# Convolution of a gated cross-attention block: four summands per output position instead of two go from GpSimd to the identity products on TensorE

## The reference

```
kv = vr[:, :, :, None, :] * x2r[:, :, None, :, :]        # (B, 16, i=8, j=8, 256)
y = irfft(rfft(kv, n=512) * rfft(k, n=512))[..., :256]     # causal convolution with k
y = y + kv * skip
out = einsum('bhijl,bhil->bhjl', y, x1r)                  # sum over the eight i
x = x + tanh(g) * out.reshape(B, 128, 256)
```

## Time and profile before

| what | value |
|---|---|
| median of three executions | 913.87 us |
| span of the profiled execution | 913.1 us |
| its median's distance from that span | 0.8 us |
| stage A, up to the last a_sum's start | 0 to 171.66 us |
| from there to the first matmul of the experts | 171.66 to 179.94 us |
| the rest | 179.94 to 913.10 us |
| mean granted TensorE clock | 0.957 of full |

### The profile page before, as it was taken

How to read it: one execution, slowest core, us unless ns; L and a number is a source line. 1 busy time by engine, 2 the same in 40 slices (tenths; PEclk the granted TensorE clock), 3 DMA queues, 4 the chain that set the end, 5 groups by cost and what they waited for, 6 DMA issues and landing times.

```text
span 913.1 us, 13862 instructions
## 1 busy us (share of the span) xinstructions
PE 823.8 (90%) x4659; PEld 653.9 (72%) x4675; DVE 619.3 (68%) x1196; ACT 320.9 (35%) x515; POOL 173.7 (19%) x185
## 2 busy tenths in 40 slices
PE   2888888699999999999998999987789999999994
PEld 2565666588888878888884555555678888888883
DVE  5999999564565465466547778788256685867754
ACT  2120212123433342342334776756243332324221
POOL 1899999400000000020000100100010010100000
PEclk9999999899999999999999999997579999999997
DMA  7221211000000000001001122110000000000000
GB/s 266 70 87 46 72 45 62 18 1 1 1 0 0 0 0 0 0 0 35 15 1 47 52 56 73 52 39 1 0 1 0 1 12 12 0 23 0 23 1 24
DMA packets 20437, 25.93 MB, mean 28 GB/s; under 512 B 3632, under 2 KB 15920, under 8 KB 20272
## 3 DMA queue, kind: packets, MB, share of 16 engines
q1 hardware_dynamic: 20400, 25.47, 8.7%
HBM read 23.36 MB, written 2.10 MB: 28 GB/s over the span
## 4 chain that ended last, share of the span: by engine, by line
PE 72%; DVE 17%; issue 6%; ACT 2%; POOL 1%; DMA 1%; DVEq 0%; SPq 0%; POOLq 0%; ACTq 0%
PE bank L1556 24%; PE bank L1426 19%; PE bank L1439 10%; PE bank L1477 5%; PE bank L1487 2%; DVE A L854 2%; DVE A L843 2%; PE bank L1565 2%; PE bank L1497 1%; PE bank L1351 1%; DVE small L1048 1%; DVE A L1058 1%; PE bank L1352 1%; PE bank L1353 1%; PE bank L1478 1%
## 5 line engine op out<-in xcount | busy, mean ns | idle before, releaser
L1556 PE MATMUL bank<-R 128*128 128x512 f32 (+4 forms) x1104 | 220.0, 360 | 9.7 <-DVE R L1210 4.9
L1556 PEld LDWEIGHTS bank<-R 128*128 128x128 f32 (+2 forms) x1104 | 180.7, 185 | 48.5 <-DVE R L1210 5.1
L1426 PE MATMUL bank<-R 128*128 128x512 f32 (+1 forms) x816 | 198.0, 392 | 1.9 <-issue 1.9
L1426 PEld LDWEIGHTS bank<-R 128*128 128x128 f32 (+1 forms) x816 | 146.7, 185 | 33.2 <-issue 2.1
L995 DVE TENSOR_TENSOR A<-bank,A 128x512 f32<-128x512 f32 (+1 forms) x68 | 47.0, 691 | 118.7 <-PE bank L1426 118.7
L1439 PEld LDWEIGHTS bank<-R 128*128 128x128 f32 (+1 forms) x816 | 105.8, 190 | 10.8 <-issue 4.0
L1439 PE MATMUL bank<-R 128*128 128x256 f32 (+1 forms) x816 | 109.4, 283 | 2.5 <-DVE R L1006 2.1
L558 ACT ACTIVATE A<-bank 128x512 f32<-128x512 f32 (+1 forms) x68 | 40.7, 599 | 194.7 <-PE bank L1426 194.7
L1477 PE MATMUL bank<-A 128*128 128x512 f32 x128 | 70.9, 636 | 0.8
L1351 PE MATMUL bank<-A 128*128 128x256 f32 x128 | 45.4, 439 | 26.0 <-DVE A L843 17.9
L430 POOL TENSOR_TENSOR A<-A 128x256 f32<-128x256 f32 x64 | 64.1, 1002 | 11.5 <-DVE A L854 11.5
(11 more groups left out here) (170 smaller groups left out, 1138.4 us busy)
## 6 DMA issues: line engine op xcount, KB each, us to landing
A<-in_w SPq DMA_DIRECT2D x17, 384.0 KB, 3.1
A<-in_w SPq DMA_DIRECT2D x8, 480.0 KB, 3.7
A<-in_ctx_one SPq DMA_DIRECT2D x8, 272.0 KB, 3.6
A<-in_ctx_half SPq DMA_DIRECT2D x8, 256.0 KB, 3.1
A<-in_ctx_nat SPq DMA_DIRECT2D x4, 512.0 KB, 3.6
A<-in_ctx_t SPq DMA_DIRECT2D x128, 16.0 KB, 2.0
out<-X SPq DMA_DIRECT2D x4, 512.0 KB, 2.9
A<-in_filt SPq DMA_DIRECT2D x1, 1536.0 KB, 11.8
```

The lines of the kernel that those rows point to most:

```text
L1426: mm = nc.tensor.matmul(dst[0:pr], wX[:, j, at + k * P:at + k * P + pr], mX[:, k], start=(n == 0), stop=(n == 5))
L1556: mm = nc.tensor.matmul(dst, a, m, start=start and n == 0, stop=stop and n == len(prods) - 1, skip_group_check=skip)
```

## The change

GpSimd makes one addition a head, from eight summands to four, straight into `z2`, which takes the place of `zh` too (`z4` is all `z2`, four parts of 128 positions for each q). The second addition and its semaphore are gone. `a_sum` multiplies four parts with the identity in place of two: 32 matmuls a group in place of 16. `a_z(h)` waits for `z2_ready` of head h - 2, and the one addition of head 0 now waits for `o_ready`.

```diff
-HALF, QUARTER = I0 // 2, I0 // 4
+HALF = I0 // 2
...
-        zh = z4[:, 0:2 * 8 * HALF * I0].rearrange("p (u q i j) -> p u q i j", u=2, q=8, i=HALF)
-        z2 = z4[:, 8 * QUARTER * P:].rearrange("p (q i t) -> p q i t", q=8, i=QUARTER)
+        z2 = z4.rearrange("p (q i t) -> p q i t", q=8, i=HALF)
...
                 pool.wait_ge(z_ready, 1 + NH0 * g + h + 1)
-
-                pool.wait_ge(z2_ready, 1 + NH0 * g + max(h - 1, 0))
-                nc.gpsimd.tensor_tensor(zh[:, u], zr[:, u, :, 0:HALF, :], zr[:, u, :, HALF:, :], ALU.add
-                                        ).then_inc(zh_ready, 1)
-                pool.wait_ge(zh_ready, 1 + NH0 * g + h + 1)
                 if h == 0:
                     pool.wait_ge(o_ready, 1 + 2 * g)
-                nc.gpsimd.tensor_tensor(z2[:, :, :, h * I0:(h + 1) * I0], zh[:, u, :, 0:QUARTER, :],
-                                        zh[:, u, :, QUARTER:, :], ALU.add).then_inc(z2_ready, 1)
+                nc.gpsimd.tensor_tensor(z2[:, :, :, h * I0:(h + 1) * I0], zr[:, u, :, 0:HALF, :],
+                                        zr[:, u, :, HALF:, :], ALU.add).then_inc(z2_ready, 1)
...
                 if not first:
-                    dve.wait_ge(zh_ready, NH0 * g + h)
+                    dve.wait_ge(z2_ready, NH0 * g + h)
...
-                        for i in range(QUARTER):
+                        for i in range(HALF):
                             mm = nc.tensor.matmul(OB[:, b * D + k * P:b * D + (k + 1) * P], z2[:, k * BG + b, i, :],
-                                                  ident[:], start=(i == 0), stop=(i == QUARTER - 1),
+                                                  ident[:], start=(i == 0), stop=(i == HALF - 1),
                                                   skip_group_check=True)
```

More of the change, by code:

```diff
@@ L268, in flamingo_kernel @@
             sem("vtp_ready"), sem("vT_ready"), sem("bvx_ready"), sem("w_ready"), sem("t_done"))
-        zh_ready = sem("zh_ready")
         kv_ready, y_ready, z_ready, z2_ready, o_ready, a_done = (
@@ L396, in _ @@
         def _(pool):
-            for counted in (y_ready, z_ready, zh_ready, z2_ready, o_ready, a_done, h_ready, down_done, b_done,
+            for counted in (y_ready, z_ready, z2_ready, o_ready, a_done, h_ready, down_done, b_done,
                             o_read, pv_done, ch_ready, ddown_done, w_mixed, dn_ready, d_done):
```

## The result

The changed kernel takes 918.45 us (median of 4 runs, 916.44 to 920.93) against 913.96 us of the kernel before on the same chip (4 runs, 913.12 to 914.47): a ratio of 1.0053, interval 1.0031 to 1.0075. It is slower by 4.5 us. The forecast was 920.3 us, its own range 918 to 923, the range over all cases 916 to 926.

A forecast was written before the change was run, and what follows sets the result against it. VectorE's queue was taken to set stage A's pace. Three turns at +1.8 us, the last group +1.4 and the start -0.4 gave +6.4 on a 913.1 us span; median 920.3 us, own range 918 to 923, all cases 916 to 926.

The forecast's parts named there:

- where the added work lands: Between heads 1 and 2 of the next group, a_z(2) waits for a_sum: +3.73 us less 0.1 slack a turn.
- Head 5's split: GpSimd's weight split behind head 5 starts 0.46 us earlier without the second addition; with shifted collisions 0.55 us a turn returned.
- rival 1: No relief: VectorE's collisions only move to other instructions; +14.2 us, 928 us; chance 0.10.
- The bias product: VectorE's L862 (1.82 us), held by a late GpSimd addition, gets back 0.45 us a turn.
- Head 10's split: GpSimd's weight split behind head 10 starts 0.46 us earlier, and VectorE's tiny instruction ending with it gains 0.46 us.
- Rival 2: GpSimd's one addition takes 0.91 us, not 0.72: +1.9 us a turn, 927.8 us in all; chance 0.04.
- The last group: Removed addition ahead of a_sum -0.45, router instructions and two splits -1.85, added matmuls +3.73: +1.4 us.
- 3.73 us and not twice that: Last a_sum: the added 32 records lie behind the clock's recovery to 2.4 GHz, so they cost +3.73 us.
- rival 5: Last group's clock: added matmuls at 1.2 GHz, 924 us, or keeping TensorE at 2.4 GHz, 918.6; chance 0.05 each.
- The start: Group 0 ahead of its head 3: L869 no longer ends behind a second addition of 0.45 us; -0.4 us.
- rival 3: More relief, in proportion to GpSimd's unhindered work: 2.8 us a turn, +3.4 in all, 917.3 us; chance 0.15.
- rival 4: Faster: the second addition's whole 7.3 us a turn comes off VectorE, 901 us; chance 0.03, 0.03 more for no change.

The follow-up runs named there:

- The experiment with the matmuls alone: Kernel before with a_sum's loop doubled over the same two parts, GpSimd keeping both additions: 927.52 us, ratio 1.0152.
- The kernel with two parts: Changed kernel with a_sum reading only two of its four parts, half of the summands left out: 906.24 us, ratio 0.9917.
- the splits moved: Kernel before with the weight splits of heads 5 and 10 ahead of the head's second GpSimd addition instead of behind it: 909.33 us, ratio 0.996.
- the splits moved and the wait in the last group alone: Kernel before, splits of heads 5 and 10 ahead of the second addition; last group's first addition of head h waits for a_kv(h + 2): 907.63 us.
- the wait everywhere: Kernel before with GpSimd's first addition of head h waiting until a_kv(h + 2) is over, in all groups: 909.05 us, ratio 0.9954.

## Why the prediction was right, and where it was not

**What bounds the kernel, and where the added work lands: right.** VectorE's queue sets the pace, a_z(2) had almost no slack behind a_sum, and the added matmuls came out at the place named. Term by term in the second turn: added 3.40 us (head 0 to head 2: +2.03 + 1.37), predicted 3.63. a_sum grew by 7.31 - 3.73 = 3.58 us as computed; the path from its end to a_z(2) is 1.33 us where it was 1.51, so 0.18 of it was slack, where 0.1 had been judged. The experiment with the matmuls alone gives 3.38, with the same 0.18.

**The relief: right in sum, nearly right in place.** In the changed kernel it is 1.37 + 0.36 = 1.73 us a turn for a predicted 1.85:
- Head 5's split: 0.49 between head 5 and head 7, after a loss of 0.28 up to head 5; net 0.21 for the predicted 0.55. The loss was named as a possibility (rival 1) and left out of the sum: an addition that is issued at once holds a_kv up.
- The bias product: 0.27 for 0.45. It takes 1.27 us instead of 1.82, and a tiny instruction ahead waits, as foreseen. Both are in the timeline at head 8, which answers to the earlier trace rows:

```profile
78.65 0.70 DVE L795 TENSOR_SCALAR ve<-mv 128x4 f32<-128x4 f32 x1
...
79.26 1.27 DVE L855 SCALAR_TENSOR_TENSOR A<-A,bias_c 128x1024 f32<-128x1024 f32 x1
```

- Head 10's split: 0.53 up to head 12 for 0.46, and 0.36 more up to head 15 that the prediction didn't have. In the timeline, beside the earlier trace rows:

```profile
83.00 0.68 DVE L836 TENSOR_TENSOR A<-A 128x512 f32<-128x512 f32 x1
83.09 1.18 POOL L428 TENSOR_TENSOR A<-A 128x256 f32<-128x256 f32 x1 [0.70 <-DVE A L847]
83.60 0.69 DVE L808 TENSOR_TENSOR tmp<-tmp,ve 128x4 f32<-128x4 f32 x1
...
84.21 0.68 DVE L847 TENSOR_TENSOR A<-bank,A 128x512 f32<-128x512 f32 x1
84.23 1.81 POOL L419 TENSOR_TENSOR R<-A,R 128x768 f32 x1
...
84.81 1.25 DVE L810 TENSOR_SCALAR tmp<-tmp 128x4 f32<-128x4 f32 x1
```

The split now starts beside a_z, where L435 stood, and the instruction that ends with it takes 1.25 us in place of 1.77. L808 ends with the addition after 0.69 us, as L815 did: the removal takes nothing off such a wait. That is why 9.6 us less of GpSimd's work in a turn gave VectorE only 1.73 us.
- Head 15's split: 0.53 us earlier at head 1, swallowed by the wait behind it. Predicted as 0. The kernel with two parts loses most of it at the same place (-1.90 at head 1, -1.55 at head 2), since there too head 2's matmuls stand behind a_sum.
- a_kv(4): 0.36 for 0.4. The reason given, that GpSimd clears its queue while VectorE waits, is enough: the experiment with the matmuls alone shows it without any removed addition. The removed addition is enough too: the kernel with two parts has it without the long wait.

**The one addition: right.** 717 ns at its shortest, as L430; the runs of 8 cost nothing. Rival 2 (0.91 us) falls.

**The last group: right up to a_sum** (-2.14 for -2.3). The five router instructions that ended with an L435 take 0.18 us in place of 0.44, 1.3 us together for the predicted 1.25; from head 15 to a_sum it is 0.53 us less for 0.45; the two splits and all else come to 0.3 us, half of the predicted 0.6. **Mis-sized at a_sum itself.** The step "3.73 us and not twice that" took the half clock of the earlier trace rows as given and put +3.73 on top; measured is +1.94, since the clock stayed at 1.00. That is the better side of rival 5, but not for rival 5's reason, that the added matmuls keep the clock up: the kernel before with the same 64 records fell to 0.50 inside its last a_sum and took 9.04 us, and the kernel with one addition and 32 records kept the full clock (3.84 us). What goes along with the full clock is GpSimd's single addition. Without L435 at its end TensorE is idle for 1.94 us ahead of the last a_sum (2.08 in one kernel), and all seven profiled executions with one addition ran it at 1.00. Of the seven with two additions, idle for 2.11 to 2.73 us there, five fell to 0.50 on the way, and two did not. The idle time does not settle it alone; the splits moved, then the splits moved and the wait in the last group alone, and the wait everywhere:

```profile
166.29 3.84 PE L1365 MATMUL bank<-ident,A 128*128 128x128 f32 x32 [2.73 <-POOL A L437]
```
```profile
164.82 3.84 PE L1367 MATMUL bank<-ident,A 128*128 128x128 f32 x32 [2.60 <-POOL A L439]
```
```profile
167.40 5.38 PE L1367 MATMUL bank<-ident,A 128*128 128x128 f32 x32 [2.60 <-POOL A L439]
```

The first has the very wait of the earlier trace rows and not its half clock; the second and the third differ in clock after the same idle time. What else decides it was not tried, so the cause of this term stays open.

**The start: a gain that can't be put down to the change.** -1.30 for -0.4. The kernel with more matmuls, whose GpSimd work is that of before, has its head 3 at 27.95 us, earlier still. The start varies between executions with the input's arrival (0.67 us of the 1.30 are a gate activation at 6.56 instead of 7.23 us), and the predicted -0.4 can't be told apart from that.

**The sum.** Without the start, the profile has 1.81 + 1.67 + 1.70 - 2.14 + 1.94 = +5.0 us, for a predicted 3 x 1.8 + 1.4 = +6.8; 1.8 of the difference is the clock in the last a_sum. The medians say +4.5 and +5.9. No relief (rival 1, 928 us) is refuted by the experiment with two parts, 7.7 us below the kernel before; relief in proportion to GpSimd's work (rival 3, 2.8 us a turn) and more of it (rival 4, 3.6 and up) by its turns, at most 1.91 us shorter.

**What the prediction did not see** is that the order of the work weighs nearly as much as its amount. Removing an addition of 0.45 us from each head gave back about 1.8 us a turn, and 7.7 us of the whole. Moving two splits and leaving all the additions in place gave 1.5 us a turn, and 6.2 us of the whole with the late addition in the last group.

## What to carry to other kernels

Count added work where the queues join: 3.6 us of it, on an engine with 6 us to spare in the turn, cost 3.4 us, because all of it stood in one piece ahead of the one result that the next engine's queue waits for. Where two engines exclude each other, read which instruction runs beside which before taking work away: an addition that runs beside an instruction with an input in PSUM is free. Here two changes of order gave 6.2 us with nothing removed, where removing one addition from each head gave 7.7. And judge a change of some 5 us in 900 by repeated runs, since two profiles of one kernel differed by 3.2 us in code that it doesn't concern.

## What the runs showed of the hardware

- VectorE's a_z (128x512, one input in PSUM) never waited for GpSimd: 650 to 692 ns in the kernel before. A four-column instruction with all inputs in SBUF took 0.15 us beside no addition, 0.41 us where it ended with GpSimd's short addition and 0.69 us where it ended with the long one. (The Trainium skill, SBUF — State Buffer, "Who interferes with whom", has that rule; these rows agree with it.)
- VectorE instructions with a single input, in SBUF, were seen both free and held in the kernel before: bn_stats (L792) took 0.41 us in each of a turn's four cases, beside additions too, while a four-column TENSOR_SCALAR (L817) took 0.15 us or, beside a split, 1.77. So "all inputs in SBUF" is too wide as the prediction has it. (The section excepts the two-port modes from its rule for one SBUF input, which the prediction leaves out; no run shows the mode of an instruction.)
- Output in runs of 8 columns costs a GpSimd addition nothing: 717 ns at 256 columns, with such an output or an unbroken one.
- 32 identity products of 128x128 in float32 (64 records) took 7.31 us at the full clock, 0.114 us a record; 16 of them (32 records) took 3.84 us in the last group where the granted clock stayed at 1.00, and 5.36 to 5.47 us where it fell to 0.50 on the way.
